# Softmax attention on one Trainium2 core: transposing the probabilities in 32x32 blocks through device memory instead of on TensorE

## What is computed

```python
def _L0_attn_b_ref(x, W_q, W_k, W_v, W_o):
    import jax, jax.numpy as jnp
    import numpy as np
    D_MODEL = 512
    B, S = (2, 512)
    scale = 1.0 / jnp.sqrt(jnp.asarray(x.shape[-1], x.dtype))
    Q = jnp.einsum('bsd,de->bse', x, W_q)
    K = jnp.einsum('bsd,de->bse', x, W_k)
    V = jnp.einsum('bsd,de->bse', x, W_v)
    scores = jnp.einsum('bqe,bke->bqk', Q, K) * scale
    attn = jax.nn.softmax(scores, axis=-1)
    out = jnp.einsum('bqk,bke->bqe', attn, V)
    return jnp.einsum('bse,ed->bsd', out, W_o)
```

## Time and profile before

| what | us |
|---|---|
| median of 3 runs (945.80 to 946.06) | 945.85 |
| the profiled execution, as timed | 945.55 |
| its span in the trace | 943.8 |
| stage B, from the first `query` to the last `attend` (468.3 to 729.1 of the span) | 260.8 |
| PE busy over the span | 930.4 |
| DVE, ACT, POOL busy over the span | 608.2, 445.3, 425.9 |

### The profile page before, as it was taken

One profiled execution on the slowest core, in us unless ns is written; L12 is line 12 of the kernel. 1 busy time (PEld: TensorE's weight loads), 2 busy tenths in 40 slices (PEclk: granted clock), 3 DMA queues, 4 the chain that ended last, 5 costly groups with the idle time before them and its releaser, 6 DMA issues.

```text
span 943.8 us, 13107 instructions
## 1 busy us (share of the span) xinstructions
PE 930.4 (99%) x4654; PEld 525.6 (56%) x4670; DVE 608.2 (64%) x1148; ACT 445.3 (47%) x884; POOL 425.9 (45%) x447
## 2 busy tenths in 40 slices
PE   7999999999999999999999999999999999999998
PEld 4888988888734444444444455444455444444444
DVE  7555656949777777767655466446466777766643
ACT  4443334356577634663333354323455686246620
POOL 5433424377357654665630043304333466545530
PEclk9999999999999999999999999999999999999999
DMA  9501300024211190015500000000000001910001
GB/s 314 181 11 34 134 23 23 1 91 135 68 66 45 23 157 1 1 23 81 107 14 1 1 1 1 1 1 1 1 1 1 1 1 23 186 59 1 1 34 56
DMA packets 115008, 44.97 MB, mean 48 GB/s; under 512 B 101952, under 2 KB 102272, under 8 KB 114688
## 3 DMA queue, kind: packets, MB, share of 16 engines
q1 hardware_dynamic: 114944, 44.13, 18.1%
HBM read 32.56 MB, written 11.57 MB: 47 GB/s over the span
## 4 chain that ended last, share of the span: by engine, by line
PE 93%; DVE 2%; ACT 1%; POOL 1%; DMA 1%; SPq 1%; issue 1%; DVEq 0%; POOLq 0%
PE psum L2211 54%; PE psum L2458 14%; PE psum L2460 13%; PE psum L2608 7%; PE psum L2619 1%; DMA bq_col<-bq 1%; PE psum L2260 1%; PE psum L2345 1%; PE psum L2249 1%; ACT probs L1417 0%; DVE xb_lo L2116 0%; ACT xb_hi L1423 0%; DVE ln_bn L1532 0%; POOL wvT_lo L1007 0%; SPq L686 0%
## 5 line engine op out<-in xcount | busy, mean ns | idle before, releaser
L972 POOL TENSOR_TENSOR hid<-hid,hid_hi 128x512 f32<-128x512 f32 x88 | 102.9, 1170 | 110.1 <-DVE hid_hi L1888 110.1
L2458 PE MATMUL psum<-xf,w_gu 128*128 128x512 f16 x352 | 133.8, 380 | 0.1
L2458 PE MATMUL psum<-xf,w_s 128*128 128x512 f16 x264 | 100.1, 379 | 1.5 <-DVE up L1861 1.3
L2460 PE MATMUL psum<-xf,w_gu 128*128 128x512 f16 x264 | 100.0, 379 | 0.0
L2211 PE MATMUL psum<-wd_low,hid_lo 128*128 128x512 bf16 (+1 forms) x330 | 73.8, 373 | 0.2
L1286 ACT ACTIVATE hid_lo<-hid 128x512 f16<-128x512 f32 x88 | 54.9, 624 | 33.3 <-POOL hid L972 33.3
L968 POOL TENSOR_TENSOR hid<-up,gate 128x512 f32<-128x512 f32 x44 | 56.1, 1274 | 25.2 <-ACT gate L1281 25.2
L2460 PE MATMUL psum<-xq,w_s 128*128 128x512 f16 x176 | 66.7, 379 | 0.0
L2458 PEld LDWEIGHTS psum<-xf,w_gu 128*128 128x128 f16 x352 | 34.3, 97 | 54.6 <-ACT acc L1271 15.5
L1281 ACT ACTIVATE gate<-gate,sg_xs 128x512 f32<-128x512 f32 x44 | 31.7, 721 | 58.4 <-DVE gate L1871 58.4
L2211 PEld LDWEIGHTS psum<-wd_low,hid_lo 128*128 128x128 f16 x330 | 32.3, 98 | 36.8
(11 more groups left out here) (336 smaller groups left out, 2430.8 us busy)
## 6 DMA issues: line engine op xcount, KB each, us to landing
turned<-blocks SPq DMA_DIRECT2D x36, 128.0 KB, 3.0
cla_wide<-cla_dram SPq DMA_DIRECT2D x16, 256.0 KB, 3.3
out<-xres SPq DMA_DIRECT2D x15, 256.0 KB, 2.0
xres<-x SPq DMA_DIRECT2D x3, 1024.0 KB, 13.0
blocks<-xn SPq DMA_DIRECT2D x24, 128.0 KB, 3.1
codes_gu<-gateT SPq DMA_DIRECT2D x1, 2816.0 KB, 11.5
codes_gu<-upT SPq DMA_DIRECT2D x1, 2816.0 KB, 10.6
codes_da<-downT SPq DMA_DIRECT2D x1, 1536.0 KB, 6.7
```

Source lines behind the costliest of these rows:

```text
L972: nc.gpsimd.tensor_tensor(hid[:, :], hid[:, :], hid_part(hid_hi, j, half), ALU.subtract).then_inc(rest_done, 1)
L2458: nc.tensor.matmul(bank(use[0]), w, x_operand(piece, k, False), start=start and k == 0, stop=False, skip_group_check=not start)
L2460: last = nc.tensor.matmul(bank(use[0]), w, x_operand(piece, k, True), start=False, stop=k == 1, skip_group_check=not start)
```

## The change

The eight PE transposes of each of the 16 rows are gone (`turn_probs`, `turn_use`). In their place DVE transposes 32x32 blocks of the row in place (`p_blocks`), SP writes the row out in four DMAs, waits for them and reads it back into the same buffer in four DMAs (`probs_turned`). `pT_high` on ACT and `pT_low` on DVE then read SBUF where they read PSUM. So a row's buffer stays occupied until `pT_low` of that row is done, and `part_sum` for the next pair waits for that (`probs_free`).

Pieces 2, 5 and 3 now have banks 5, 2 and 3 of their own. Piece 5 is no longer in one bank with piece 3, so DVE adds it a second time, into the even row (`half_done`). The order on PE becomes: pieces 1, 2, 6, 5, 3 of the next pair, `attend` of the even row, pieces 7 and 4, then queries or `turn_both`, and `attend` of the odd row. For pair 0 three `values` come ahead of the scores in batch 0 and one in batch 1, where there were six.

Beside this the high and low parts of even rows get tiles of their own (`even_hi`, `even_lo`), one set of temporaries moves by 1280 bytes, and since the new tiles lie where two of the F2 weight sums were kept, POOL makes four such sums again (two early, two late) where it made three.

```diff
+VALUES_FIRST = (3, 1)
 ...
     def score_use(piece, p):
         return {1: (4, 4 * p), 6: (4, 4 * p + 1), 7: (4, 4 * p + 2), 4: (4, 4 * p + 3),
-                2: (5, 3 * p), 5: (5, 3 * p + 1), 3: (5, 3 * p + 2)}[piece]
-
-    def turn_use(b, i):
-        return (4, 16) if (b, i) == (1, BT - 1) else (2, i)
+                2: (5, p), 5: (2, p), 3: (3, p)}[piece]
 ...
+            def probs_turned(b, i):
+
+                n, t = b * BT + i, probs[i % 2]
+                sp.wait_ge(p_blocks_done, n + 1)
+                src = t[:, :].rearrange("p (m j) -> p m j", j=SQ)
+                for a in range(QUADS):
+                    sp.dma_start(prob_blocks[n, a].rearrange("m (c i) j -> i (m c) j", c=QUADS),
+                                 src[a * SQ:(a + 1) * SQ, :, :]).then_inc(p_out[i % 2], 16)
+                sp.wait_ge(p_out[i % 2], p_all(b, i))
+                dst = t[:, :].rearrange("p (m a j) -> p m a j", a=QUADS, j=SQ)
+                for a in range(QUADS):
+                    sp.dma_start(dst[:, :, a, :],
+                                 prob_blocks[n, a].rearrange("m p j -> p m j")).then_inc(p_moved[i % 2], 16)
 ...
                 def part_sum(piece, p):
 ...
+                    if probs_free(b, 2 * p + row) > 0:
+                        act.wait_ge(pT_lo_done, probs_free(b, 2 * p + row))
                     nc.scalar.activation(cols(probs[row], half), bank(4), ACT.Copy).then_inc(drained[4], 1)
 ...
                 def pT_high(i):
-                    use = turn_use(b, i)
-                    u.full(use)
-                    nc.scalar.activation(pT(b, i)[0], bank(use[0], 2).rearrange("p (g n) -> p g n", g=2), ACT.Copy,
+                    act.wait_ge(p_moved[i % 2], p_all(b, i))
+                    if i > 1:
+                        u.full(out_use(b, i - 2))
+                    nc.scalar.activation(pT(b, i)[0], probs[i % 2][:, :].rearrange("p (g n) -> p g n", g=2), ACT.Copy,
                                          scale=PS).then_inc(pT_hi_done, 1)
 ...
+                def p_blocks(i):
+                    dve.wait_ge(probs_done, b * 8 + (i + 1))
+                    nc.vector.transpose(probs[i % 2][:, :], probs[i % 2][:, :]).then_inc(p_blocks_done, 1)
 ...
-                def turn_probs(i):
 ...
-                    for t in range(BT):
-                        last = nc.tensor.transpose(bank(use[0], 2)[:, t * P:(t + 1) * P],
-                                                   probs[i % 2][:, t * P:(t + 1) * P], ident[:, :])
-                    last.then_inc(filled[use[0]], 1)
 ...
                     if t0 == 0:
-                        u.read_out(turn_use(b, i))
+                        pe.wait_ge(pT_lo_done, b * 8 + i + 1)
 ...
+                def first_row(p):
+                    for piece in (1, 2, 6, 5, 3):
+                        score(piece, p)
+
+                def second_row(p):
+                    score(7, p)
+                    score(4, p)
+
                 if b == 0:
                     for n in range(4):
                         query(0, 0, n)
-                for i in range(6):
+                for i in range(VALUES_FIRST[b]):
                     values(i)
-                for piece in (1, 2, 6, 5, 7):
-                    score(piece, 0)
+                first_row(0)
+                for i in range(VALUES_FIRST[b], 6):
+                    values(i)
+                second_row(0)
                 values(6)
-                score(3, 0)
-                score(4, 0)
                 values(7)
                 for p in range(4):
 ...
+                    if p < 3:
+                        first_row(p + 1)
+                    attend(2 * p)
+                    if p < 3:
+                        second_row(p + 1)
+                    if p == 0:
+                        for n in range(4):
+                            query(b, 1, n)
+                    elif p < 3:
+                        turn_both(2 * p - 2)
+                    elif b == 0:
+                        for n in range(4):
+                            query(1, 0, n)
+                    attend(2 * p + 1, 0, 6)
+                    if p in (1, 2):
+                        turn_both(2 * p - 1)
+                    attend(2 * p + 1, 6, 8)
```

More of the change, by code:

```diff
@@ L816, in _ @@
                     weights_back()
+                    for b in range(BATCHES):
+                        for i in range(BT):
+                            probs_turned(b, i)
             store(0, *range(BT))
@@ L1434, in _ @@
                     s_high(0, 0, 1)
-                for i in range(1, 6):
+                for i in range(1, VALUES_FIRST[b]):
                     v_high(i)
@@ L2148, in _ @@
                 part_add(3, 0)
                 row_max(0)
+                for i in range(VALUES_FIRST[b], 6):
+                    v_low(i)
+                    if i == VALUES_FIRST[b]:
+                        p_blocks(0)
+                if b == 1:
+                    x_stats(q, 0)
+                    x_stats(q, 1)
+                part_add(5, 0)
                 row_max(1)
+                v_low(6)
+                p_blocks(1)
                 v_low(7)
+                x_stats(q, 2)
+                x_stats(q, 3)
@@ new lines, in _ @@
+                    if p < 3:
+                        p_blocks(2 * p + 2)
+                    if p == 0:
+                        x_stats(q, 6)
+                        x_stats(q, 7)
+                    pT_low(2 * p + 1)
+                    if p == 1:
+                        x_normalise(q, 0)
+                    out_add(2 * p)
+                    if p < 3:
+                        part_add(5, p + 1)
+                        row_max(2 * p + 3)
+                        p_blocks(2 * p + 3)
@@ L2591, in score @@
                     use, n = score_use(piece, p), q_n(b, p // 2, 1)
-                    start = piece in (1, 2, 5)
+                    start = piece in (1, 2, 5, 3)
                     if piece == 1:
```

249 lines of the change are left out of this document (91 added, 158 removed).

## The result

The changed kernel takes **980.95 us** (median of 4 runs, 978.9 to 984.86) where the kernel before takes 945.83: a ratio of **1.0377**, 95% interval 1.0344 to 1.041. It is slower, as forecast, and 10 us above the forecast of 971. The profiled execution took 984.86 (span 983.0), 3.9 above the median and above the forecast range of 958 to 983, which the median is in; that of before took 945.55.

The account below looks back on a forecast made before the run. PE alone was taken to set stage B's length (busy 260.4 of 260.8 us). 945.55 less 14.8 for removed transposes plus 40.6 of new PE waits, the ledger of steps, gave 971.3; forecast 971 us, range 958 to 983.

Parts of the forecast that it names:

- (a): Piece 4 follows piece 7 in bank 4: PE waits for the bank's round trip, 0.85 us in pair 0.
- (b): Piece 4, pair 1: piece 7's copy needs row 1's low part, queued late on DVE; wait 3.9 us.
- (c): Pairs 2 and 3: piece 7's copy waits for pT_low behind the next row's exponential and block transpose; 1.3 us, twice.
- (d): Piece 6, pair 1: bank 4 needs piece 1's copy, hence pT_low(0), queued late on DVE; wait 2.8 us.
- (e): Values behind pair 0's scores wait for a v_low whose v_high stands behind row 0's exponential; 0.6 us.
- (f): Piece 6, pair 2, waits for pT_low(2), whose high part stands behind the copies of the queries; 0.5 us.
- (g): Second turn_both of pairs 2 and 3 waits for xn from DVE; 3.5 and 3.1 us.
- (h): Piece 6, pair 3, waits for piece 1's copy, on ACT behind x_34_high(1); 1.3 us.
- (i): attend(6) waits 0.2 us; attend(7) in batch 1 waits 1.8 us, its row starting its DMAs last without queries as cover.
- the two waits of 3.9: PE's clock falls only after these two waits in stage B: 975.7 us, a case inside the forecast.
- all eight long ones: Rival: after each of eight waits of 2.8 to 3.9 us, ten matmuls run at the lower clock: +17.6, 989; chance 0.05.
- the DMAs bind: Rival: the rows' DMA landings come as late as their upper ends, 976 to 983 us; chance 0.15.

Follow-up runs that it names:

- e3: The kernel before with 4 of each row's 8 transposes left out on TensorE: 940.3 us, ratio 0.9941.
- e1: The changed kernel without the 128 DMAs of probabilities, the high part following the block transpose at once: 982.89 us, ratio 1.0384.
- e2: The changed kernel with six x_stats a batch moved out of the chains to later places on DVE: 969.39 us, ratio 1.0256.
- e6: e5 with four more edits of the lists of ACT and DVE, TensorE's order untouched: 963.78 us, ratio 1.0195.
- e5: e2 with x_normalise for the second turn_both of pairs 2 and 3 put ahead of the block transpose and x_second: 975.29 us, ratio 1.0308.
- e4: The changed kernel with 128 matmuls of no use put into TensorE's waits: 980.88 us, ratio 1.0374.
- e10_five_rows: e6 with piece 4 in bank 3, further list edits, and 5 of 16 rows turned on TensorE again, 11 through memory: 941.39 us, ratio 0.9958.

## Why the prediction was right, and where it was off

**Direction and cause: right.** PE set the stage before, the gain taken was 14.8 (for half of it e3 measured 6.9 of the expected 7.25, its new waits allowed for), and the new order put PE behind chains on ACT and DVE. e1 shows that the DMAs are no part of it, e2 that places in a list are.

**The sum of the waits: right, with errors that cancel.** 40.1 measured for 40.6. By step:

| step | forecast | measured |
|---|---|---|
| (a) piece 4, pair 0 | 0.85 | 0.78 |
| (b) piece 4, pair 1 | 3.9 | 3.67 |
| (c) piece 4, pairs 2 and 3 | 1.3 each | 1.14 each |
| (d) piece 6, pair 1 | 2.8 | 2.75 |
| (e) values | 0.6 | 0.56 |
| (f) piece 6, pair 2 | 0.5 | 1.49 and 1.78 |
| (g) second turn_both, pairs 2 and 3 | 3.5 and 3.1 | 2.14 three times, 1.93 once |
| (h) piece 6, pair 3 | 1.3 | 2.82 |
| (i) attend(6) | 0.2 | 1.72 and 0.41 |
| (i) attend(7), batch 1 | 1.8 | 0.70 |

The steps that counted a chain of priced links from a row, (a) to (e), are within 0.25. In (a) two things are mixed: the 0.85 had the 0.16 of the pipeline's end in it, so as a gap it was 0.69 for 0.78, and the difference is PE's start behind ACT's copy, 0.14 us after its end (504.00 behind 503.86) where I took 0.05. (f) was taken for the queue behind the copies of the queries; e6, which among other edits puts the high part of row 2 ahead of the last of them, has no wait there. (g) was 2.3 too dear in a batch, (f) 1.0 to 1.3 too cheap, (h) 1.5, `attend(6)` up to 1.5. My ledger treated (g), (h) and (i) as separate terms, but they hang together, as e5 shows: what is taken off at (g) reappears at (h) and (i). So too much at the one and too little at the others made a sum that fits better than its parts. Step (i) also named a wrong cause for `attend(7)`: without any DMA it waits the same 0.7, for its turn on ACT and DVE behind the copies of x. ACT comes to the high part of that row straight from the copies, without waiting for a landing:

```profile
759.41 0.63 ACT L1146 ACTIVATE xf<-x_last 128x512 f16<-128x512 f32 x1 [0.86 <-POOL x_last L877]
760.00 1.06 ACT L1458 ACTIVATE xb_hi<-probs 128x1024 f16<-128x1024 f32 x1
```

e4 and e6 show the cause that I named, in kernels where PE is earlier.

**The step that missed the 10 us** (14 in the profiled execution) is the sum. It took the ledger at its gaps and gave the clock nothing.
- The end of the pipeline: 0.16 for each of 26 waits, 4.2 us. I had it in the price of the bank's round trip and in no other step.
- The clock. I had priced a fall at 2.2 and forecast it only for the two waits of 3.9, as an upper case inside the forecast (975.7), or for all eight long ones (989, chance 0.05). It came five times in the profiled execution, once for 6.8 us, and cost 9.7. It stood at waits of 2.75, 3.67 (twice), 2.82 and 1.93, so not only at the longest. Nor did it come each time: batch 0 and batch 1 have the same 2.75 at piece 6 of pair 1 and the same 2.82 at piece 6 of pair 3, and each was followed by a fall in one of the two only. Nor is it all a net cost. After the fall at 752.8 `attend(6)` starts 4.53 us after the second `turn_both`, the same as in e1 and e2, which have no fall there but wait 1.71 instead of 0.41: the low part of row 6 was not ready before. The fall at 732.3 cost its full 1.7: from piece 6 to piece 4 of pair 3 it is 13.35 us, and 11.65 in batch 0, where there is none. So what the falls cost in the end is less than 9.7; e4, nearly without them, is 4.4 shorter in the profiled execution and level in the median.

With both, 971.3 + 4.2 + 9.7 = 985.2 for the profiled 984.86; the median is 3.9 lower, which no run explains. The five falls agree in kind with "The HAM clock gate" in TensorE: Matmul & The Clock Gate of the Trainium skill: an array that idles is granted half its clock until it has been busy again. The prediction gave that rule too small a chance.

**The rest.** Weight sums cost nothing (F2 as long as before). Stage B was forecast 286 us long and is 300; the waits at ACT's copies were forecast as 23 and are 27.8, at xn 13 and are 8.4. The rival "the DMAs bind" (976 to 983) holds the median, but for a reason that e1 refutes; and since the upper bound of the range was drawn from the landings, it is luck that the median lies within it. The estimate of 4.6 us out and back from the Trainium skill does not bear on these DMAs: the section gives its figure for DMAs that GpSimd issues, and here SP issues them, at 9.0 to 11.3 us from the block transpose to the copy.

## What to carry to other kernels

Work taken off a saturated engine is gained only if the replacement's results are asked for later than its whole chain, and on engines that work down a list the chain includes everything queued ahead of each link; statistics and preparation that nobody waits for belong into the gaps and not between two links. Price a wait of TensorE at its gap plus the end of the pipeline, and, once waits of 2 us and more stand in a stage, reckon with stretches at the lower clock; a part of what they take can be waited for anyway. Waits along one chain are one term: removing the first moves it to the next, so change the last link or send back to the old way just those pieces whose cover is too short.

## What the runs showed of the hardware

- The falls of TensorE's granted clock in stage B stand at waits of 1.9 to 5.3 us, in nine traces, and each lasted 3.4 us or 6.8 us. e10_five_rows, with no wait above 1.8, had none in the profiled execution. The changed kernel's mean was 0.990 to 0.991 in all four runs. With its waits filled with matmuls of no use it was 1.000 in one run and 0.997 to 0.998 in three. Which wait is followed by a fall is not the same from one execution to the next: in e1_no_way, with the same waits, the stretch at 531 lasted 3.4 us and the one at 753 did not come.
- Where e2_stats_late and e5_xn_ahead have nearly equal waits in sum (33.4 and 32.8), the one with fewer and longer waits had 17.1 us at the lower clock for 6.8, and a median 5.9 us higher.
- Four DMAs of 128 KB out and four back, in pieces of 128 bytes, took 9.0 to 11.3 us from the end of the block transpose to the copy, wherever the copy waited for them (e6 to e10 and e4), for a forecast of 9.9. Their medians from issue to landing in the changed kernel:

```profile
prob_blocks<-probs SPq DMA_DIRECT2D x64, 128.0 KB, 2.7
probs<-prob_blocks SPq DMA_DIRECT2D x64, 128.0 KB, 2.9
```
